# Rounding and subtracting a unit's transposed probabilities in one instruction each

## Chip, cores and metric

The kernel runs on one core of one Trainium2 chip. The metric is the device time of one execution in microseconds; the median of three runs of the kernel before is 1191.67 us (1191.44 to 1194.56).

## What is computed

A decoder of two layers on 512 tokens of width 512 (two sequences of 256). Each step is added to a residual stream `x` after a layer norm: an autocorrelation mix, a quantised cross product with a context, a quantised feed-forward, a grouped-query attention over a gathered key cache, a cross attention over context and latents, and a mixture of eight experts. The change touches the two attentions, which end in

```python
# first: 32 heads, 8 key heads, width 128, 512 cached + 256 new keys
scores = jnp.einsum('bhld,bhtd->bhlt', qh, k_full) / math.sqrt(HD)
attn = jax.nn.softmax(scores, axis=-1)
out = jnp.einsum('bhlt,bhtd->bhld', attn, v_full)
# second: 16 heads, 4 key heads, width 96, 512 context + 256 latent keys
scores = jnp.einsum('bkgqd,bksd->bkgqs', q, k) * scale
attn = jax.nn.softmax(scores.astype(jnp.float32), axis=-1).astype(q.dtype)
out = jnp.einsum('bkgqs,bksd->bkgqd', attn, v)
```

## The kernel before

Every engine (TensorE: PE, ScalarE: ACT, VectorE: DVE, GpSimd: POOL, SyncE: SP) has its own program, written out by hand in the order in which it runs; the engines meet only at semaphores (`s["name"]`), and a wait holds up everything behind it on its engine. Products of full precision are made of three matmuls each (`product`, L1887 to L1889): every operand is split into a rounded part, made by ScalarE as a copy into a rounded type, and a remainder, made by VectorE or GpSimd as a subtraction.

An attention runs over groups, one for each key head: eight groups (0 to 7) in the first attention, four in the second. A group has 16 units: four heads times four tiles of 128 query rows, each against 768 keys. Unit U = 16 g + u goes through the engines like this:

- TensorE, two units ahead: the scores (six matmuls, L1887 to L1889) into one of two pairs of banks.
- VectorE: the row maximum out of PSUM (`row_max`, L1464). ScalarE: the exponential with its row sum (`exps`, L969). VectorE: the reciprocal (`row_sum`, L1469). GpSimd: the product of the two (L673).
- TensorE: the probabilities, 128 x 768, are transposed in six steps of 128 columns (L2018), three into bank 4 and three into bank 5 (`B_PT`).
- ScalarE rounds them into `PTH` (L984); VectorE subtracts the rounded part from PSUM into `PTL` (L1514). Each does this for half a unit, one bank, at a time. The transposes of the next unit overwrite the banks, so each half of them waits for the subtraction of the same half (`pt_out0`, `pt_out1`).
- After the transposes TensorE has other matmuls to do in most units: values times probabilities of a whole head (`head_values`), the next group's queries (`project_q`), the output projection of the group before (`project_out`).

In unit u TensorE's order is: scores of U+2, transposes of U, other matmuls. ScalarE's order is: the roundings of U, a finished head's or query's copy where there is one, the exponential of U+2. VectorE's order is: a low query part (L1479) where one is due, the maximum of U+2, the subtractions of U, the reciprocal of U+2, then rotations of queries (L1445, L1447), a head's remainder (`head_out`, L1485) or the addition of a projected row block (L1491). The tables at the top of the kernel (`Q_UNITS`, `V_UNITS`, `Q_OUT`, `Q_SPLIT`, `V_OUT` and the same with a 2 for the second attention) say in which unit each extra step lies. The first group of an attention has no output projection and no earlier head behind it, and the last one has no queries of a next group.

Of the kernel before, what the change touches and what calls it, by code (L numbers as in the profile page):

```python
# [20 lines left out]
P = 128  # L21
B, S, D = 2, 256, 512
TOK = B * S
RT = TOK // P
# [20 lines left out]
UNITS = GH * RT  # L45
# [27 lines left out]
def decoder_kernel(nc, x, ctx, ctx_t, qscale, wgu, wd, dft, idft, nyq, freqs, wq1, wk1, wv1, wo1,  # L73
                   kcache, vcache, block_idx, wq2, wk2, wv2, wo2, gate_w, expert_w, out):
    es = ExitStack()
    with es:
# [206 lines left out]
        def bank(n):  # L283
            return PS[:, n, :]

        def bankb(n):
# [24 lines left out]
            sc_ready nmax_ready exp_done rsum_ready pn_ready pt_psum pt_out1 pt_out0 ot_psum ot_ev  # L311
# [78 lines left out]
        def fr(ap):  # L390
            return ap.bitcast(FR)
# [11 lines left out]
        def _(sp):  # L403
# [174 lines left out]
            sp.wait_ge(s["pt_psum"], 2 * UNITS * KV1)  # L578
# [133 lines left out]
        def _(act):  # L712
# [229 lines left out]
            def attention(first, groups, rotated, hd, new_values_out, prepare):  # L942
# [29 lines left out]
                def group(g, tail, last):  # L972
                    for u in range(UNITS):
# [8 lines left out]
                        for half in range(2):  # L982
                            act.wait_ge(s["pt_psum"], 2 * U + half + 1)
                            act.activation(fr(PTH[:, (u // 4) % 2, 3 * half:3 * half + 3, u % 4 * P:(u % 4 + 1) * P]),  # L984
                                           bank(B_PT[half])[:, 0:3 * P].rearrange("p (k c) -> p k c", k=3),
                                           ACT.Copy).then_inc(s["pt_hi"], 1)
# [108 lines left out]
        def _(dve):  # L1095
# [362 lines left out]
            def attention(first, groups, rotated, hd, first_rows, last_queries, prepare):  # L1458
# [36 lines left out]
                def group(g, tail, last):  # L1495
                    for u in range(UNITS):
# [14 lines left out]
                        for half in range(2):  # L1511
                            ks = slice(3 * half, 3 * half + 3)
                            dve.wait_ge(s["pt_hi"], 2 * U + half + 1)
                            dve.tensor_tensor(fr(PTL[:, (u // 4) % 2, ks, cols]),  # L1514
                                              bank(B_PT[half])[:, 0:3 * P].rearrange("p (k c) -> p k c", k=3),
                                              PTH[:, (u // 4) % 2, ks, cols], ALU.subtract)\
                               .then_inc(s[f"pt_out{half}"], 1)
# [125 lines left out]
        def _(pe):  # L1643
# [257 lines left out]
            def attention(first, groups, hd, keys, new_values, first_product=None):  # L1901
# [9 lines left out]
                def head_values(g, j, k0=0, k1=KK):  # L1911

                    if k0 == 0:
                        pe.wait_ge(s["pt_out1"], UNITS * g + RT * (j + 1))
                        pe.wait_ge(s["pt_out0"], UNITS * g + RT * (j + 1))
                        pe.wait_ge(s["ot_ev"], GH * g + j)
# [17 lines left out]
                def last_head_values(g, half):  # L1934

                    j = GH - 1
                    if half == 0:
                        pe.wait_ge(s["pt_out1"], UNITS * (g + 1))
                        pe.wait_ge(s["pt_out0"], UNITS * (g + 1))
# [56 lines left out]
                def group(g, tail, last):  # L1996
                    for u in range(UNITS):
# [13 lines left out]
                        pe.wait_ge(s["pn_ready"], U + 1)  # L2011
                        for half in range(2):
                            pe.wait_ge(s[("pt_out0", "pt_out1")[half]], U)
# [6 lines left out]
                            mm.then_inc(s["pt_psum"], 1)  # L2020
# [265 lines left out]
```

## Time and profile before

| | |
|---|---|
| median of the runs | 1191.67 us (1191.44 to 1194.56) |
| the profiled execution | 1190.17 us, its span 1188.3 us |
| PE (matmuls) busy | 1104.0 us, 93% of the span |
| DVE busy | 869.3 us, 73% |
| ACT busy | 607.1 us, 51% |
| POOL busy | 491.7 us, 41% |
| first attention, transposes of units | 262.7 to 785.4 us of the span |
| second attention, transposes of units | 833.4 to 1069.7 us |

The page of a profile adds up what each engine did over the whole span. What an engine waits for, and whether that matters, is read from the views of single stretches: the instructions in order of time with the idle time ahead of each, the chain of waits followed back from the last instruction, and busy time by stretch. Times in those views are counted from the start of the span.

### The profile page before, as it was taken

Reading aid. Unit: us, or ns where it says so; the run is one execution under the profiler, and the core shown is the slowest. Engines: PE = TensorE matmul, PEld = TensorE weight load, DVE = VectorE, ACT = ScalarE, POOL = GpSimd, SP = SyncE. Lnnn points to the kernel's source line nnn. Section 1 sums busy time; section 2 is a strip of 40 time slices with the busy share of each in tenths; the row PEclk is TensorE's granted clock in tenths of the full one; section 3 lists DMA queues with packets and bytes.
Section 4 is the critical chain, followed back from the end, with each engine's and each line's share of the span. In section 5 each row is a group of like instructions: output and inputs, shape, how many; then the busy total and the mean of one; then the engine's idle time right before and its main releaser. Section 6 shows DMA issues by size and latency. Waiting matters only on the chain.

```text
span 1188.3 us, 17689 instructions
## 1 busy us (share of the span) xinstructions
PE 1104.0 (93%) x5871; PEld 882.5 (74%) x5878; DVE 869.3 (73%) x1471; ACT 607.1 (51%) x1236; POOL 491.7 (41%) x360
## 2 busy tenths in 40 slices
PE   3976867899999999999999999999899999999998
PEld 2433333477888888888888888877788989887887
DVE  6999989867867777786868777657676676755434
ACT  2523443436656556565656656553665666553110
POOL 1361000124655645564655545462656565550000
PEclk9798989899999999999999999999999999999999
DMA  9364145220011011101010010142103020111121
GB/s 320 131 200 163 49 129 190 76 85 27 18 50 36 23 53 31 53 18 57 18 57 26 22 35 14 62 106 63 61 18 92 18 60 31 48 36 72 71 106 71
DMA packets 41813, 83.10 MB, mean 70 GB/s; under 512 B 10212, under 2 KB 18917, under 8 KB 38565
## 3 DMA queue, kind: packets, MB, share of 16 engines
q1 hardware_dynamic: 40164, 77.24, 20.1%
q0 software_dynamic: 1600, 5.24, 1.4%
q8 instruction: 28, 0.46, 0.2%
q14 instruction: 21, 0.16, 0.0%
HBM read 71.59 MB, written 10.22 MB: 69 GB/s over the span
## 4 chain that ended last, share of the span: by engine, by line
PE 79%; DVE 12%; issue 4%; ACT 3%; POOL 1%; DMA 1%; SPq 0%; ACTq 0%; DVEq 0%; POOLq 0%
PE PS L1887 21%; PE PS L1889 20%; PE PS L1888 20%; PE PS L2018 9%; PE PS L1704 1%; PE PS L1830 1%; PE PS L1784 1%; ACT arena L969 1%; PE PS L1654 1%; ACT PTH L984 1%; PE PS L1815 1%; PE PS L1673 1%; DVE arena L1238 1%; DVE arena L1115 1%; DVE arena L1126 1%
## 5 line engine op out<-in xcount | busy, mean ns | idle before, releaser
L673 POOL TENSOR_TENSOR arena<-arena,rsum 128x768 f32<-128x768 f32 x192 | 283.1, 1475 | 362.3 <-DVE rsum L1469 362.3
L984 ACT ACTIVATE PTH<-PS 128x384 fp32r<-128x384 f32 x384 | 167.8, 489 | 245.3 <-PE PS L2018 245.0
L1464 DVE TENSOR_REDUCE nmax<-PS 128x1 f32<-128x768 f32 x192 | 182.9, 953 | 116.6 <-PE PS L1889 115.3
L1514 DVE TENSOR_TENSOR PTL<-PS,PTH 128x384 fp32r<-128x384 f32 x384 | 194.3, 547 | 7.8 <-ACT PTH L984 7.2
L969 ACT ACTIVATE arena<-PS,nmax 128x768 f32<-128x768 f32 x192 | 174.3, 908 | 33.5 <-DVE nmax L1464 33.2
L2018 PE MATMUL PS<-identf,arena 128*128 128x128 f32 x1152 | 158.3, 273 | 6.8 <-POOL arena L673 3.4
L2018 PEld LDWEIGHTS PS<-identf,arena 128*128 128x128 f32 x1152 | 130.2, 140 | 10.1 <-POOL arena L673 5.5
L658 POOL TENSOR_TENSOR WQL<-arena,WQH 128x512 fp32r<-128x512 f32 x44 | 59.1, 1345 | 63.9 <-ACT WQH L743 63.9
L1887 PE MATMUL PS<-PTH,VSH 128*128 128x512 f32 (+1 forms) x198 | 81.0, 409 | 2.4 <-DVE OTL L1485 2.0
L1889 PE MATMUL PS<-PTH,VSL 128*128 128x512 f32 (+1 forms) x198 | 76.4, 386 | 0.0
L1887 PE MATMUL PS<-WOH,OTH 128*128 128x512 f32 (+1 forms) x180 | 74.2, 412 | 2.1 <-DVE OTL L1485 2.0
L1888 PE MATMUL PS<-PTL,VSH 128*128 128x512 f32 (+1 forms) x198 | 76.0, 384 | 0.0
L1887 PE MATMUL PS<-HTH,WQH 128*128 128x512 f32 x176 | 73.6, 418 | 1.6 <-issue 1.6
L1469 DVE RECIPROCAL rsum<-psum_exp 128x1 f32<-128x1 f32 x192 | 31.5, 164 | 59.5 <-ACT arena L969 52.3
L1888 PE MATMUL PS<-WOL,OTH 128*128 128x512 f32 (+1 forms) x180 | 71.0, 394 | 0.0
L1889 PE MATMUL PS<-WOH,OTL 128*128 128x512 f32 (+1 forms) x180 | 70.8, 394 | 0.0
L658 POOL TENSOR_TENSOR WOL<-arena,WOH 128x512 fp32r<-128x512 f32 (+1 forms) x48 | 70.0, 1458 | 0.0
L1889 PE MATMUL PS<-HTH,WQL 128*128 128x512 f32 x176 | 69.7, 396 | 0.0
L1888 PE MATMUL PS<-HTL,WQH 128*128 128x512 f32 x176 | 69.5, 395 | 0.0
L1479 DVE TENSOR_TENSOR QTL<-arena,QTH 128x512 fp32r<-128x512 f32 x37 | 62.4, 1686 | 9.6 <-ACT QTH L961 9.6
L1887 PE MATMUL PS<-PTH,VH 128*96 128x256 f32 x192 | 56.3, 293 | 3.5 <-DVE OTL L1485 3.5
L1889 PE MATMUL PS<-PTH,VL 128*96 128x256 f32 x192 | 54.0, 281 | 0.0
(289 smaller groups left out, 2535.1 us busy)
## 6 DMA issues: line engine op xcount, KB each, us to landing
arena<-in_wo SPq DMA_DIRECT2D x12, 1024.0 KB, 4.8
arena<-in_wq SPq DMA_DIRECT2D x44, 256.0 KB, 2.6
arena<-in_expert_w SPq DMA_DIRECT2D x8, 1024.0 KB, 4.8
arena<-in_wgu SPq DMA_DIRECT2D x11, 512.0 KB, 5.3
arena<-v_dram SPq DMA_DIRECT2D x8, 384.0 KB, 3.4
arena<-in_wd SPq DMA_DIRECT2D x4, 704.0 KB, 6.0
arena<-in_ctx SPq DMA_DIRECT2D x4, 512.0 KB, 3.5
arena<-in_ctx_t SPq DMA_DIRECT2D x2, 1024.0 KB, 11.0
```

The costliest lines, as they stand in the source:

```text
L658: pool.tensor_tensor(fr(lo), raw, hi, ALU.subtract).then_inc(s["w_ready"], heads)
L673: pool.tensor_tensor(PR[:, u % 4, :], PR[:, u % 4, :], rsum[:, u % 4:u % 4 + 1].broadcast_to([P, KEYS]), ALU.mult).then_inc(s["pn_ready"], 1)
L969: act.activation(PR[:, slot, :], SC[pair][:, 0:KEYS], ACT.Exp, bias=nmax[:, slot:slot + 1], accum_out=psum_exp[:, slot:slot + 1]).then_inc ...
L984: act.activation(fr(PTH[:, (u // 4) % 2, 3 * half:3 * half + 3, u % 4 * P:(u % 4 + 1) * P]), bank(B_PT[half])[:, 0:3 * P].rearrange("p (k ...
L1464: dve.tensor_reduce(nmax[:, slot:slot + 1], SC[pair][:, 0:KEYS], AX.X, ALU.max, negate=True)\
L1469: dve.reciprocal(rsum[:, slot:slot + 1], psum_exp[:, slot:slot + 1]).then_inc(s["rsum_ready"], 1)
L1479: dve.tensor_tensor(fr(QTL[:, j, :]), QT[:, j, :], QTH[:, j, :], ALU.subtract)\
L1514: dve.tensor_tensor(fr(PTL[:, (u // 4) % 2, ks, cols]), bank(B_PT[half])[:, 0:3 * P].rearrange("p (k c) -> p k c", k=3), PTH[:, (u // 4) % ...
L1887: pe.matmul(out, fr(xh), fr(yh), start=start, stop=False)
L1888: pe.matmul(out, fr(xh), fr(yl), start=False, stop=False)
L1889: return pe.matmul(out, fr(xl), fr(yh), start=False, stop=stop)
L2018: mm = pe.transpose(bank(B_PT[half])[:, k * P:(k + 1) * P], PR[:, u % 4, c * P:(c + 1) * P], identf[:])
```

## The change

The two roundings of a unit become one ScalarE instruction that reads both banks, and the two subtractions one VectorE instruction. The semaphore that tells of finished transposes (`pt_psum`) counts units now and not halves, `pt_hi` likewise, and one of the two signals of the subtraction (`pt_out0`) is gone. The waits that counted halves are rewritten to match, among them one of SP's ahead of the load of a weight of the second attention.

```diff
-            sp.wait_ge(s["pt_psum"], 2 * UNITS * KV1)
+            sp.wait_ge(s["pt_psum"], UNITS * KV1)
...
-                        for half in range(2):
-                            act.wait_ge(s["pt_psum"], 2 * U + half + 1)
-                            act.activation(fr(PTH[:, (u // 4) % 2, 3 * half:3 * half + 3, u % 4 * P:(u % 4 + 1) * P]),
-                                           bank(B_PT[half])[:, 0:3 * P].rearrange("p (k c) -> p k c", k=3),
-                                           ACT.Copy).then_inc(s["pt_hi"], 1)
+                        act.wait_ge(s["pt_psum"], U + 1)
+                        act.activation(fr(PTH[:, (u // 4) % 2, :, u % 4 * P:(u % 4 + 1) * P]
+                                          .rearrange("p (a k) c -> p a k c", a=2)),
+                                       PS[:, B_PT[0]:B_PT[1] + 1, 0:3 * P].rearrange("p a (k c) -> p a k c", k=3),
+                                       ACT.Copy).then_inc(s["pt_hi"], 1)
...
-                        for half in range(2):
-                            ks = slice(3 * half, 3 * half + 3)
-                            dve.wait_ge(s["pt_hi"], 2 * U + half + 1)
-                            dve.tensor_tensor(fr(PTL[:, (u // 4) % 2, ks, cols]),
-                                              bank(B_PT[half])[:, 0:3 * P].rearrange("p (k c) -> p k c", k=3),
-                                              PTH[:, (u // 4) % 2, ks, cols], ALU.subtract)\
-                               .then_inc(s[f"pt_out{half}"], 1)
+                        dve.wait_ge(s["pt_hi"], U + 1)
+                        lo, hi = (t[:, (u // 4) % 2, :, cols].rearrange("p (a k) c -> p a k c", a=2) for t in (PTL, PTH))
+                        dve.tensor_tensor(fr(lo), PS[:, B_PT[0]:B_PT[1] + 1, 0:3 * P]
+                                          .rearrange("p a (k c) -> p a k c", k=3), hi, ALU.subtract)\
+                           .then_inc(s["pt_out1"], 1)
...
                         pe.wait_ge(s["pn_ready"], U + 1)
+                        pe.wait_ge(s["pt_out1"], U)
                         for half in range(2):
-                            pe.wait_ge(s[("pt_out0", "pt_out1")[half]], U)
                             if not tail and u == 0:
                                 pe.wait_ge(s["vn_ev"], v_steps + half + 1)
                             for k in range(3):
                                 c = 3 * half + k
                                 mm = pe.transpose(bank(B_PT[half])[:, k * P:(k + 1) * P],
                                                   PR[:, u % 4, c * P:(c + 1) * P], identf[:])
-                            mm.then_inc(s["pt_psum"], 1)
+                        mm.then_inc(s["pt_psum"], 1)
```

On TensorE, unit 15 of a middle group of the first attention stands like this before (`pn_ready` tells of GpSimd's product; `identf` is the identity that transposes):

```order
L1889 MATMUL PS<-KNH,QTL 128x256
L2018 MATMUL PS<-identf,arena 128x128 [waits pt_out0,pn_ready]
L2018 MATMUL PS<-identf,arena 128x128 x2
L2018 MATMUL PS<-identf,arena 128x128 [waits pt_out1]
L2018 MATMUL PS<-identf,arena 128x128 x2
L1887 MATMUL PS<-HTH,WQH 128x512 [waits w_ready]
```

and like this after:

```order
L1887 MATMUL PS<-KNH,QTL 128x256
L2014 MATMUL PS<-identf,arena 128x128 [waits pt_out1,pn_ready]
L2014 MATMUL PS<-identf,arena 128x128 x5
L1885 MATMUL PS<-HTH,WQH 128x512 [waits w_ready]
L1886 MATMUL PS<-HTL,WQH 128x512
```

The wait of the second three transposes has moved ahead of the first three.

On VectorE, unit 14 of such a group, from the low query part on, before (`pt_hi` tells of the rounding, `sc_ready` of the scores, `exp_done` of the exponential):

```order
L1479 TENSOR_TENSOR QTL<-arena,QTH 128x512 [waits q_hi]
L1463 REGISTER_ALU
L1464 TENSOR_REDUCE nmax<-PS 128x1 [waits sc_ready]
L1513 ISA
L1514 TENSOR_TENSOR PTL<-PS,PTH 128x3x128 [waits pt_hi]
L1513 REGISTER_ALU
L1514 TENSOR_TENSOR PTL<-PS,PTH 128x3x128 [waits pt_hi]
L1469 RECIPROCAL rsum<-psum_exp 128x1 [waits exp_done]
```

and after:

```order
L1479 TENSOR_TENSOR QTL<-arena,QTH 128x512 [waits q_hi]
L1463 REGISTER_ALU
L1464 TENSOR_REDUCE nmax<-PS 128x1 [waits sc_ready]
L1513 TENSOR_TENSOR PTL<-PS,PTH 128x6x128 [waits pt_hi]
L1469 RECIPROCAL rsum<-psum_exp 128x1 [waits exp_done]
```

Two subtractions of three blocks have become one of six, with one wait; what stands around them is in the same order.

## Rows read from the trace of the kernel before

**Rows 1.** Windows: us, then busy us (instructions) per engine, clock, DMA share, GB/s.

```profile
core 0: us, PE busy (x) PEld busy (x) DVE busy (x) ACT busy (x) POOL busy (x), PEclk, DMA share, GB/s
330.00:740.00 410.00, 410.00 (x2223) 350.52 (x2222) 309.19 (x517) 247.10 (x522) 224.24 (x153) 1.00 0.12 36
```

**Rows 2.** Groups by line and shape: busy us, mean ns of one, idle before them.

```profile
L1514 DVE TENSOR_TENSOR PTL<-PS,PTH 128x384 fp32r<-128x384 f32 x384 | 194.3, 547 | 7.8 <-ACT PTH L984 7.2
L1464 DVE TENSOR_REDUCE nmax<-PS 128x1 f32<-128x768 f32 x192 | 182.9, 953 | 116.6 <-PE PS L1889 115.3
L969 ACT ACTIVATE arena<-PS,nmax 128x768 f32<-128x768 f32 x192 | 174.3, 908 | 33.5 <-DVE nmax L1464 33.2
L984 ACT ACTIVATE PTH<-PS 128x384 fp32r<-128x384 f32 x384 | 167.8, 489 | 245.3 <-PE PS L2018 245.0
...
L1005 ACT ACTIVATE VSH<-arena 128x768 fp32r<-128x768 f32 x8 | 6.8, 850 | 0.0
```

**Rows 3.** Instructions in order of time, unit 8 of group 7: start, us, idle before.

```profile
762.45 0.82 PE L2018 MATMUL PS<-identf,arena 128*128 128x128 f32 x6
...
762.97 0.87 ACT L984 ACTIVATE PTH<-PS 128x384 fp32r<-128x384 f32 x2 [2.03 <-PE PS L2018]
...
763.52 1.01 DVE L1514 TENSOR_TENSOR PTL<-PS,PTH 128x384 fp32r<-128x384 f32 x2
...
764.22 0.92 PE L2018 MATMUL PS<-identf,arena 128*128 128x128 f32 x6
766.14 0.47 PE L1887 MATMUL PS<-PTH,VSH 128*128 128x512 f32 x1 [1.01 <-DVE OTL L1485]
```

**Rows 4.** Chain of waits, the same place: start us, us, what.

```profile
758.82 0.66 PE PS L2018 x6
...
762.61 0.34 PE PS L2018 x3
762.97 0.87 ACT PTH L984 x2
...
765.41 0.60 DVE OTL L1485
```

**Rows 5.** Instructions in order of time, units 12 to 15 of group 1.

```profile
382.94 0.88 ACT L984 ACTIVATE PTH<-PS 128x384 fp32r<-128x384 f32 x2 [1.30 <-PE PS L2018]
...
385.31 0.16 DVE L1469 RECIPROCAL rsum<-psum_exp 128x1 f32<-128x1 f32 x1 [0.81 <-ACT arena L969]
...
387.05 0.96 DVE L1464 TENSOR_REDUCE nmax<-PS 128x1 f32<-128x768 f32 x1
...
389.31 1.47 POOL L673 TENSOR_TENSOR arena<-arena,rsum 128x768 f32<-128x768 f32 x1 [1.03 <-DVE rsum L1469]
...
389.59 1.73 DVE L1479 TENSOR_TENSOR QTL<-arena,QTH 128x512 fp32r<-128x512 f32 x1 [0.36 <-ACT QTH L961]
...
390.00 0.82 PE L2018 MATMUL PS<-identf,arena 128*128 128x128 f32 x6
...
392.11 1.00 DVE L1514 TENSOR_TENSOR PTL<-PS,PTH 128x384 fp32r<-128x384 f32 x2
...
393.13 0.82 PE L2018 MATMUL PS<-identf,arena 128*128 128x128 f32 x6
...
396.24 0.81 PE L2018 MATMUL PS<-identf,arena 128*128 128x128 f32 x6
```

**Rows 6.** TensorE in order of time, at its idle stretches in both attentions.

```profile
287.78 0.47 PE L1887 MATMUL PS<-HTH,WQH 128*128 128x512 f32 x1 [1.46 <-issue]
...
784.56 0.92 PE L2018 MATMUL PS<-identf,arena 128*128 128x128 f32 x6 [0.94 <-DVE PTL L1514]
...
840.98 0.82 PE L2018 MATMUL PS<-identf,arena 128*128 128x128 f32 x6
...
854.13 0.88 PE L2018 MATMUL PS<-identf,arena 128*128 128x128 f32 x6 [2.31 <-POOL arena L673]
...
952.38 0.36 PE L1887 MATMUL PS<-PTH,VH 128*96 128x256 f32 x1 [0.49 <-DVE OTL L1485]
...
1071.70 0.47 PE L1887 MATMUL PS<-WOH,OTH 96*128 96x512 f32 x1 [2.00 <-DVE OTL L1485]
```

More of the change, by code:

```diff
@@ L310, in decoder_kernel @@
             ot_half ot_half_hi ot_half_ev q_moved ot_moved q_psum q_cos q_ready vn_psum vn_ev
-            sc_ready nmax_ready exp_done rsum_ready pn_ready pt_psum pt_out1 pt_out0 ot_psum ot_ev
+            sc_ready nmax_ready exp_done rsum_ready pn_ready pt_psum pt_out1 ot_psum ot_ev
             y_psum y_added
@@ L1914, in head_values @@
                         pe.wait_ge(s["pt_out1"], UNITS * g + RT * (j + 1))
-                        pe.wait_ge(s["pt_out0"], UNITS * g + RT * (j + 1))
                         pe.wait_ge(s["ot_ev"], GH * g + j)
@@ L1938, in last_head_values @@
                         pe.wait_ge(s["pt_out1"], UNITS * (g + 1))
-                        pe.wait_ge(s["pt_out0"], UNITS * (g + 1))
                         pe.wait_ge(s["ot_ev"], GH * g + j)
```

## The prediction

> **What bounds the kernel now.** I read first the windows by stage. From 330 to 740 us, the middle of the first attention, TensorE is busy in all 410.00 us, VectorE in 309.19 (75%), ScalarE in 247.10 (60%), and the granted clock is 1.00, the 2.4 GHz level [rows 1]. So there the matmul engine is the bound, time taken off the other two gives nothing back, and the change can only act by making TensorE wait or wait less. It takes no matmul away.
>
> Second, the rows by line and shape, for durations. A rounding of half a unit (ScalarE, L984) takes 0.489 us, a subtraction (VectorE, L1514) 0.547 us, and there are 384 of each [rows 2]. There is no 768-wide row of either. The nearest are the ScalarE copy of 768 columns out of SBUF at 0.850 us, the exponential of 768 columns out of PSUM at 0.908 us, and the VectorE reduction of 768 columns out of PSUM at 0.953 us [rows 2].
>
> Third, the loop that a unit closes, where nothing covers it. In the last group of the first attention unit 8 has no other matmuls than scores: its transposes start at 762.45, the rounding at 762.97, the subtraction at 763.52, the next unit's transposes at 764.22 [rows 3]. That is 0.52 (three transposes and the hand-over) + 0.49 (half 0 rounded) + 0.06 + 0.55 (half 0 subtracted) + 0.15 (hand-over) = 1.77 us, which is 764.22 - 762.45. A unit cannot be followed sooner.
>
> Fourth, the chain of waits, to see where this loop decides. In that group it leaves TensorE after three transposes (762.61, 0.34 us), goes through the two roundings, the exponential and the subtraction of the head's output (L1485) and comes back at 766.14, after 1.01 us of idle [rows 3, 4].
>
> **The change part by part.** The new order is six transposes, then one rounding, then one subtraction, then the next six transposes.
>
> Start. In the chain three transposes take 0.34 us and six 0.66 [rows 4]: the rounding may start 0.33 us later, 0.85 after the transposes instead of 0.52.
>
> Rounding. Removed are two instructions that together last 0.87 us [rows 4]; added is one. I take 0.85 us, the row of the same operation and width. Bounds: 0.91 (the exponential's row), and 0.80, which is the pair's 0.87 less a second start-up of 0.07 (2 x 0.489 - 0.908). So ScalarE ends 0.85 + 0.85 = 1.70 us after the start instead of 0.52 + 0.87 = 1.39: 0.31 us later (0.26 to 0.37). Everything behind it in ScalarE's order (exponential, head output, queries) starts that much later.
>
> Subtraction. The pair lasts 1.01 us [rows 3]. One instruction: 0.95 (the reduction's row); bounds 1.02 (nothing saved) and 0.88 (a start-up of 0.14 saved, 2 x 0.547 - 0.953). It ends at 1.70 + 0.06 + 0.95 = 2.71 instead of 0.52 + 0.49 + 0.06 + 1.02 = 2.09: 0.62 us later (0.50 to 0.75).
>
> Loop. The shortest distance of two units rises from 1.77 to 2.71 + 0.15 = 2.86 us (2.74 to 2.99).
>
> The two waits of the transposes become one ahead of all six. Behind it on TensorE stand the unit's value, query or output products; those wait for nothing else there, so they slip with it. One wait and one signal fewer cost nothing either way: of the six transposes 0.66 us is twice the three's 0.34 within 0.02, so no gap stood between the halves.
>
> Where it reaches TensorE, place by place:
>
> (a) The middle, units 0 to 13 and 15: the next transposes come 3.11 us or more after the last (unit 15: 396.24 - 393.13 [rows 5]), above 2.86. No cost; if the loop grew past 3.1 us these would start to pay.
>
> (b) Unit 14 of groups 0 to 6. A chain runs over three units and no link has room: rounding of unit 12 at 382.94, the exponential behind it, the reciprocal that waited 0.81 us for that exponential, two rotations, the maximum of unit 13 at 387.05 without a wait, its exponential, the rounded queries, the low query part at 389.59 which waited 0.36 us for them, another maximum, the subtraction of unit 14 at 392.11 [rows 5]. It starts 2.11 us after the transposes at 390.00; the next ones come at 393.13, 3.13 later [rows 5]. Today half 0 is free at 2.11 + 0.55 + 0.15 = 2.81, half 1 at 3.26, when the second three want it at 3.46: covered. After: 2.11 + 0.31 + 0.95 + 0.15 = 3.52, so 0.39 us of new wait (0.27 to 0.52). Seven groups: 2.7 us (1.9 to 3.6).
>
> (c) Places where TensorE already waits for what stands behind the rounding on ScalarE: group 0 of the first attention (287.78, 1.46 us idle, the end of a rotation chain that starts with unit 0's rounding) [rows 6], units 5, 8 and 11 of its last group, unit 15 of the first three groups of the second attention (952.38, idle until L1485) [rows 6], units 9 and 12 of its last. These nine pay 0.31 us each: 2.8 us (2.3 to 3.3).
>
> (d) The last unit pair of both attentions, where TensorE waits for a head subtraction queued behind the unit's own (784.56, 0.94 us idle; 1071.70, 2.00 us) [rows 6]: 0.62 each, 1.2 us (1.0 to 1.5).
>
> (e) Units 2 to 6 of the second attention's first group follow each other with scores alone: 854.13 - 840.98 = 13.15 us for five [rows 6]. Five loops of 2.86 are 14.3: 1.15 us (0.55 to 1.8). GpSimd, which ends this stretch today (2.31 us idle before 854.13), gets its reciprocals late by about the same.
>
> Sum: 2.7 + 2.8 + 1.2 + 1.15 = 7.9 us (5.8 to 10.2). The saved 0.02 us of ScalarE and 0.06 of VectorE per unit, 192 times, is 15 us of busy time and lies wholly beside TensorE.
>
> Rows 1 have VectorE at 75% and ScalarE at 60% while TensorE has no idle. The Trainium skill (Perfetto Trace Analysis, Optimizing Scalar/DVE Operations) says that grouping into larger operations helps when the engine is saturated, and that breaking instructions up may finish work sooner when ScalarE or VectorE are not saturated but cause bubbles on other engines. By its second half this change goes the wrong way; the trace agrees as far as neither engine is full. A second page (VectorE: DVE Perf Modes, the TRN2 errata) gives 172 + 768 cycles at 1.2 GHz and 120 + 768 at 0.96 GHz for these two forms, 0.78 and 0.925 us; with those as an estimate the sum would be 6.0 us.
>
> **The rivals.**
>
> The cover holds: the low query part of unit 14 (1.73 us beside a GpSimd multiplication of 1.47 that starts 0.28 us earlier [rows 5]) runs shorter once both move, so (b) vanishes, and GpSimd's order absorbs (e). For it: VectorE is that stretch's tightest engine; against: both start from the same reciprocal and move together. 7.9 - 2.7 - 1.15 = 4.0, at the low ends 3.3 us: 1195.0 to 1195.7.
>
> The wide forms cost what two narrow ones do: 0.98 and 1.09 us, no overlap, for an access that steps over two banks. Rounding 0.44 later, loop 3.13: (b) 4.6, (c) 4.0, (d) 1.8, (e) 2.5, sum 12.9: 1204.6. Against: the exponential reads both banks in one instruction at 0.908.
>
> Faster, the other side: the wait and signal between the halves cost TensorE's sequencer time in every unit that the trace folds into the transposes. It decides from (7.9 + 3.6) / 192 = 0.06 us per unit on; at 0.10 us it gives 19.2 - 7.9 = 11.3 us: 1180.4. Against: the 0.66 and 0.34 above leave 0.02.
>
> **How the numbers follow.** The profiled execution took 1190.17 us, its span 1188.3; the median of the runs is 1191.67, 1.5 more. The forecast is 1198.1 for a profiled execution and 1191.67 + 7.9 = 1199.6 for the median; its own ends are 1197.5 and 1201.9. A measurement of this kernel can tell 0.3%, 3.6 us, from no change.
> Chances: forecast 0.76, cover 0.10, wide forms 0.10, faster 0.04. The range takes in the cover's low end and a third of the wide forms' case: 1194.8 to 1203.0. Faster by over 0.3%: 0.04. Within: half of the cover's case, and 0.05 of the forecast's through scatter of the runs (those of before lie 3.1 us apart), 0.10. Slower: 0.86.
>
> **What would show it.** Right: ScalarE's form at 0.80 to 0.91 us and VectorE's at 0.88 to 1.02, 192 of each; 2.8 to 2.9 us between the two transpose groups of unit 8 in the last group; new idle of about 0.4 us before the transposes of unit 15 seven times, in a stretch that has none now, with the subtraction as what ended it; VectorE some 15 us less busy at the same TensorE work. Wrong: no idle between 330 and 740 us (the cover held), idle also before unit 0 (wide forms), or transposes of a unit that take less than 0.66 us in the chain.

## The result and the profile after

The changed kernel took 1201.32 us, the median of four executions (1197.31 to 1202.04); the kernel before, on the same chip, 1191.74. The ratio is 1.0071, with a 95% interval of 1.0053 to 1.0089: it is slower by 6 to 11 us. A second set of runs, taken with the experiments, gave 1200.39 against 1192.32 us, ratio 1.0065 (1.0050 to 1.0081). The profiled execution took 1197.31 us, its span 1195.5; before they were 1190.17 and 1188.3.

The two instructions came out as they were costed, 192 of each. Groups by line and shape of the changed kernel (count, then busy us, mean ns of one, idle before them), to set beside [rows 2]:

```profile
L1513 DVE TENSOR_TENSOR PTL<-PS,PTH 128x768 fp32r<-128x768 f32 x192 | 183.4, 955 | 72.2 <-ACT PTH L983 71.3
...
L983 ACT ACTIVATE PTH<-PS 128x768 fp32r<-128x768 f32 x192 | 156.0, 813 | 279.4 <-PE PS L2014 279.1
```

The subtraction takes 0.955 us and the rounding 0.813. VectorE is busy 10.9 us less and ScalarE 11.8 us less for these two steps than in [rows 2], and the kernel is slower all the same. Where it became slower stands in the list of what TensorE waited for between 255 and 1190 us (what for, then us in total, how often, the longest). Of the kernel before:

```profile
PE PS L1887 <- DVE OTL L1485: 7.5, 8, 2.0
PE PS L2018 <- POOL arena L673: 3.4, 3, 2.3
PE PS L2018 <- DVE PTL L1514: 3.2, 5, 1.2
```

and of the changed one:

```profile
PE PS L2014 <- DVE PTL L1513: 16.3, 21, 2.0
PE PS L1885 <- DVE OTL L1485: 4.2, 7, 2.6
PE PS L2014 <- POOL arena L673: 1.1, 1, 1.1
```

The transposes (L2014) now wait for the subtraction at 21 places instead of 5. Part of that was there before under other names: the waits for a head's output (OTL) and for GpSimd have shrunk. The three rows add up to 14.1 us before and 21.6 after, 7.5 us more. The other rows of the list shrank from 2.6 to 1.3 us, so the idle time of the whole list rose by 6.2 us. It does not hold the whole cost, as will be seen at unit 15 below.

Unit 8 of group 7 shows the loop, as in [rows 3]; instructions in order of time of the changed kernel (start, us, engine, idle before):

```profile
765.13 0.82 PE L2014 MATMUL PS<-identf,arena 128*128 128x128 f32 x6
...
765.99 0.81 ACT L983 ACTIVATE PTH<-PS 128x768 fp32r<-128x768 f32 x1 [2.09 <-PE PS L2014]
766.69 0.59 ACT L965 ACTIVATE OTH<-PS 128x512 fp32r<-128x512 f32 x1
767.17 0.91 ACT L969 ACTIVATE arena<-PS,nmax 128x768 f32<-128x768 f32 x1
...
766.83 0.96 DVE L1513 TENSOR_TENSOR PTL<-PS,PTH 128x768 fp32r<-128x768 f32 x1 [0.54 <-ACT PTH L983]
768.20 0.16 DVE L1469 RECIPROCAL rsum<-psum_exp 128x1 f32<-128x1 f32 x1 [0.41 <-ACT arena L969]
768.28 0.67 DVE L1485 TENSOR_TENSOR OTL<-PS,OTH 128x512 fp32r<-128x512 f32 x1
...
767.94 0.85 PE L2014 MATMUL PS<-identf,arena 128*128 128x128 f32 x6 [0.93 <-DVE PTL L1513]
769.10 0.47 PE L1885 MATMUL PS<-PTH,VSH 128*128 128x512 f32 x1 [0.31 <-DVE OTL L1485]
```

The rounding starts 0.86 us after the transposes (0.52 before), the subtraction 0.84 after it, and the next unit's transposes start 767.94 - 765.13 = 2.81 us after the last ones, where it was 1.77. TensorE's single wait of 1.01 us for the head's output has become 0.93 for the subtraction and 0.31 for the head's output.

In the middle of the first attention TensorE was never idle before [rows 1]. The same stretch now:

```profile
330.00:740.00 410.00, 408.95 (x2210) 348.55 (x2209) 304.85 (x417) 240.02 (x422) 223.39 (x153) 1.00 0.11 36
```

The 1.05 us that are missing belong to one place in each group, ahead of unit 15's transposes. In group 1, to set beside [rows 5] (VectorE first, then TensorE):

```profile
390.03 1.74 DVE L1479 TENSOR_TENSOR QTL<-arena,QTH 128x512 fp32r<-128x512 f32 x1 [0.35 <-ACT QTH L961]
391.69 0.95 DVE L1464 TENSOR_REDUCE nmax<-PS 128x1 f32<-128x768 f32 x1
392.56 0.94 DVE L1513 TENSOR_TENSOR PTL<-PS,PTH 128x768 fp32r<-128x768 f32 x1
...
390.17 0.82 PE L2014 MATMUL PS<-identf,arena 128*128 128x128 f32 x6
...
393.06 0.29 PE L1886 MATMUL PS<-KNL,QTH 128*128 x1
393.19 0.28 PE L1887 MATMUL PS<-KNH,QTL 128*128 x1
393.65 0.84 PE L2014 MATMUL PS<-identf,arena 128*128 128x128 f32 x6 [0.18 <-DVE PTL L1513]
```

The idle column says 0.18 us, yet the distance of the two transposes is 393.65 - 390.17 = 3.48 us and was 3.13: 0.35 more. The row of 393.19 is why: its 0.28 us is the time from its start to its modelled end, while back-to-back matmuls of this form start every 0.12 to 0.13 us (393.06 to 393.19). Idle is counted from that end, so some 0.17 us of each such wait is not in the idle column. In this kernel waits are better sized from distances between starts, and so are the sums in the next section.

### The profile page after: what moved, and what is told of

The parts are those of the page before. It is cut to its first block, busy times and chain, and to the rows that moved or that the text cites. A ratio compares the mean times of both kernels' runs of the same rounds, so it can differ in the third digit from the quotient of the medians.

```text
span 1195.5 us, 16802 instructions
## 1 busy us (share of the span) xinstructions
PE 1105.4 (92%) x5878; PEld 883.3 (74%) x5878; DVE 859.7 (72%) x1279; ACT 594.8 (50%) x1044; POOL 491.8 (41%) x360
## 4 chain that ended last, share of the span: by engine, by line
PE 74%; DVE 15%; issue 5%; ACT 5%; POOL 1%; DMA 1%; ACTq 0%; DVEq 0%; SPq 0%; POOLq 0%
PE PS L1885 19%; PE PS L1887 19%; PE PS L1886 19%; PE PS L2014 9%; ACT arena L969 2%; DVE nmax L1464 1%; PE PS L1702 1%; PE PS L1828 1%; PE PS L1782 1%; DVE PTL L1513 1%; ACT PTH L983 1%; PE PS L1652 1%; DVE arena L1445 1%; DVE arena L1447 1%; PE PS L1671 1%
## 5 line engine op out<-in xcount | busy, mean ns | idle before, releaser
L983 ACT ACTIVATE PTH<-PS 128x768 fp32r<-128x768 f32 x192 | 156.0, 813 | 279.4 <-PE PS L2014 279.1
L1513 DVE TENSOR_TENSOR PTL<-PS,PTH 128x768 fp32r<-128x768 f32 x192 | 183.4, 955 | 72.2 <-ACT PTH L983 71.3
L2014 PE MATMUL PS<-identf,arena 128*128 128x128 f32 x1152 | 157.7, 273 | 17.5 <-DVE PTL L1513 16.3
L2014 PEld LDWEIGHTS PS<-identf,arena 128*128 128x128 f32 x1152 | 129.9, 140 | 21.8 <-issue 20.4
```

The source lines that it names most:

```text
L983: act.activation(fr(PTH[:, (u // 4) % 2, :, u % 4 * P:(u % 4 + 1) * P] .rearrange("p (a k) c -> p a k c", a=2)), PS[:, B_PT[0]:B_PT[1] + 1 ...
L1513: dve.tensor_tensor(fr(lo), PS[:, B_PT[0]:B_PT[1] + 1, 0:3 * P] .rearrange("p a (k c) -> p a k c", k=3), hi, ALU.subtract)\
L2014: mm = pe.transpose(bank(B_PT[half])[:, k * P:(k + 1) * P], PR[:, u % 4, c * P:(c + 1) * P], identf[:])
```

## Where the 7 us are

The transposes of every unit have a start time in both traces, so the difference between the kernels can be followed from unit to unit. From the first transposes of the first attention to the first output product after the last unit (262.74 to 1071.70 us before, 261.09 to 1078.82 after) the changed kernel needs 8.77 us more. Of that 1.3 us are seven matmuls of group 0 that ran at TensorE's lower clock level; 7.4 us are waits:

| place | forecast, us | measured, us |
|---|---|---|
| (b) unit 14 and 15, groups 0 to 6 | 2.7 | 2.5 |
| (c) nine places behind ScalarE's order | 2.8 | 2.3 |
| (d) the last unit pair of both attentions | 1.2 | 1.4 |
| (e) units 2 to 6 of the second attention's first group | 1.15 | 1.26 |
| (a) everything else | 0 | 0.0 |
| sum | 7.9 | 7.4 |

The second profile of the changed kernel gives the same numbers within 0.05 us at each place (group 0 and its clock apart). The waits of (d) and (e) in the first one:

```profile
786.07 0.85 PE L2014 MATMUL PS<-identf,arena 128*128 128x128 f32 x6
788.90 0.85 PE L2014 MATMUL PS<-identf,arena 128*128 128x128 f32 x6 [1.98 <-DVE PTL L1513]
789.50 0.47 PE L1885 MATMUL PS<-WOH,OTH 128*128 128x512 f32 x1
...
859.33 0.88 PE L2014 MATMUL PS<-identf,arena 128*128 128x128 f32 x6 [1.12 <-POOL arena L673]
...
1078.82 0.47 PE L1885 MATMUL PS<-WOH,OTH 96*128 96x512 f32 x1 [2.58 <-DVE OTL L1485]
```

They answer to 784.56, 854.13 and 1071.70 in [rows 6], with 0.94, 2.31 and 2.00 us. At (e) the wait for GpSimd became shorter since four waits of 0.93 to 1.01 us for the subtraction now stand ahead of it; the stretch as a whole went from 13.15 to 14.41 us.

At (d) in the first attention the row of 784.56, which the prediction names, is a wait for the unit's own subtraction. The head's subtraction behind it releases the first output product, which stands in these rows of the kernel before:

```profile
782.80 0.82 PE L2018 MATMUL PS<-identf,arena 128*128 128x128 f32 x6
...
785.62 0.47 PE L1887 MATMUL PS<-WOH,OTH 128*128 128x512 f32 x1
```

From the transposes of unit 14 to that product it was 2.82 us (782.80 to 785.62) and is 3.43 (786.07 to 789.50). At the end of the second attention it went from 2.81 us, between the last transposes and 1071.70, to 3.43. So each of the two places pays 0.61 us for the head's subtraction; the rest of the 1.4 us lies close around the first place.

## Experiments: which part of the change costs

Three kernels each contain one part of the change. The first rounds both banks in one instruction and keeps the two subtractions with their two signals.

```diff
-for half in range(2):
-    act.wait_ge(s["pt_psum"], 2 * U + half + 1)
...
+act.wait_ge(s["pt_psum"], U + 1)
...
+               PS[:, B_PT[0]:B_PT[1] + 1, 0:3 * P].rearrange("p a (k c) -> p a k c", k=3),
+               ACT.Copy).then_inc(s["pt_hi"], 1)
...
-    dve.wait_ge(s["pt_hi"], 2 * U + half + 1)
+    dve.wait_ge(s["pt_hi"], U + 1)
```

> Undoes half of the change: one rounding over both banks behind six transposes, but two subtractions of half a unit each, and TensorE waits for each half apart. Theory (what counts is when ScalarE's rounding and VectorE's last subtraction end, place by place): against the kernel before, the rounding ends 0.27 us later and both subtractions 0.62 us later, half 0 is free 0.31 us earlier than in the changed kernel, so the loop is 0.85 + 0.81 + 0.04 + 0.55 + 0.15 = 2.40 us. Unit 14: half 0 free 3.08 us after its transposes, covered by 3.13; half 1 at 3.54 where it is wanted at 3.46, about 0.08 us in each of seven groups, 0.5 us. Nine places behind ScalarE's order 0.27 each, 2.4 us. Last unit pairs 0.62 each, 1.2 us. Second attention's first group: five loops of 2.40 fit into 13.15, 0 to 0.3 us. Sum about 4.3 us, ratio 1.0036. Rival one (the single subtraction with its single wait is the whole cost): within 1 us of before. Rival two (waiting with the rounding for six transposes is the whole cost): 7 us or more, as the changed kernel.

Measured: 1198.03 against 1192.32 us, ratio 1.0052 (1.0037 to 1.0066). The forecast of 4.3 us (1.0036) lies just below the interval. From the first transposes to the first output product after the last unit the profile has 5.3 us more, so neither rival (1 us; 7 us or more) fits. The loop measured 2.41 us (764.32 to 766.73) where 2.40 was expected:

```profile
764.32 0.82 PE L2018 MATMUL PS<-identf,arena 128*128 128x128 f32 x6
766.73 0.92 PE L2018 MATMUL PS<-identf,arena 128*128 128x128 f32 x6 [0.53 <-DVE PTL L1514]
```

By place it paid 0.3 us at (b), 1.6 in group 7, 0.7 at (e), where 0 to 0.3 was expected, and 2.5 in the rest of the second attention, 0.56 of it at a place where the trace names a DMA (below). Without that it is 4.7 us.

The second part alone: two roundings, one subtraction over both banks behind them, one wait of TensorE.

```diff
-for half in range(2):
-    dve.wait_ge(s["pt_hi"], 2 * U + half + 1)
...
+dve.wait_ge(s["pt_hi"], 2 * U + 2)
...
+dve.tensor_tensor(fr(lo), PS[:, B_PT[0]:B_PT[1] + 1, 0:3 * P]
+                  .rearrange("p a (k c) -> p a k c", k=3), hi, ALU.subtract)\
+   .then_inc(s["pt_out1"], 1)
...
+pe.wait_ge(s["pt_out1"], U)
 for half in range(2):
-    pe.wait_ge(s[("pt_out0", "pt_out1")[half]], U)
```

> The other half alone: two roundings of half a unit each, as before, one subtraction over both banks behind the second, one wait of TensorE ahead of six transposes. Theory: ScalarE's order is not moved, so the nine places behind it pay nothing. The subtraction starts at 1.40 + 0.05 and ends at 2.40 us after the transposes (2.09 before, 2.66 in the changed kernel); loop 2.55 us. Unit 14: 2.11 + 0.95 + 0.15 = 3.21 against 3.13, 0.08 us in each of seven groups, 0.5 us. Last unit pairs 0.31 each, 0.6 us. Five loops of 2.55 fit into 13.15. Sum about 1.1 us, ratio 1.0009. Rival one (the subtraction is the whole cost): 7 us or more. Rival two: nothing at all, within 0.5 us of before.

Measured: 1194.46 us, ratio 1.0016 (1.0008 to 1.0025), 1 to 3 us. The waits are 2.35 us: 0.6 at (b), 0.5 in group 7, 0.5 at (e), 0.8 in the rest, 0.5 of that again at the DMA's place. Without it 1.8 us, where 1.1 was expected; the 0.5 at (e) is most of what was missing. The loop measured 2.54 us, expected 2.55.

The third changes no instruction of ScalarE or VectorE; TensorE only waits for both halves ahead of all six transposes.

```diff
+pe.wait_ge(s["pt_out0"], U)
+pe.wait_ge(s["pt_out1"], U)
 for half in range(2):
-    pe.wait_ge(s[("pt_out0", "pt_out1")[half]], U)
```

> The kernel before with one edit: TensorE waits for both subtracted halves ahead of all six transposes; roundings and subtractions stay as halves. Theory: loop 2.09 + 0.15 = 2.24 us instead of 1.77, with ScalarE's and VectorE's ends unmoved by themselves. Unit 14: 2.11 + 1.01 + 0.15 = 3.27 against 3.13, 0.14 us in each of seven groups, 1.0 us; where TensorE then waits behind ScalarE's order the later transposes push the rounding behind them, at most 0.14 us at each of nine places, since half 1 waits there already; the rest fits. Sum 1.0 to 2.0 us, ratio 1.0008 to 1.0017. Rival (losing the overlap of the halves' transposes is the main cost): 5 us or more, ratio over 1.004.

Measured: 1193.48 us, ratio 1.0016 (1.0005 to 1.0026). The loop is 2.23 us, expected 2.24. The profile has 2.8 us more than before between the same two points, of which some 1.5 us lie in group 0 with a stretch at the lower clock level; the waits are about 1.3 us, 1.0 of them at unit 14 and 15 of groups 0 to 6, as expected. The rival (5 us or more) fell.

So the loop followed the ends of the instructions in every variant: 1.77, 2.23, 2.41, 2.54 and 2.81 us for the kernel before, the wait alone, the rounding alone, the subtraction alone and the whole change. The larger part of the cost comes with the rounding that waits for six transposes, 4.7 us against 1.8 for the single subtraction. About half of it, 2.3 us, lies at the nine places behind ScalarE's order, where the single subtraction alone pays nothing: ScalarE's following work moves with the rounding.

At one place of the second attention a DMA may add something to the comparison. In the profile of the subtraction alone:

```profile
905.56 0.50 PE L1885 MATMUL PS<-WOH,OTH 128*128 128x512 f32 x1 [0.25 <-DMA OTL<-OTL]
```

Three profiles have this row (both parts of the change alone and a later variant), with 0.47 to 0.56 us more between the transposes around it than before. In four other variants the same distance is 0.15 to 0.24 us longer without such a row, and in the remaining profiles, those of the two kernels compared among them, it is unchanged. What causes it stays open.

## Experiments: why the runs of one kernel differ by 4 us

The timed runs of the changed kernel lay 4 us above its profiled one. It was run again unaltered.

> The changed kernel unaltered, for a second profile: its timed runs were 4 us above its profiled one (1201.3 against 1197.3). Theory one (the granted clock falls to its lower level at some of the enlarged waits, not at the same ones in every execution): ratio 1.006 to 1.008, and the profile shows stretches at granted clock 0.50 behind waits, between 260 us and the end, that differ from those of the first profile (286 to 289 us), each some 1 to 2 us long in lost time. Theory two (the waits themselves are longer in those runs): the places before the transposes of units 14, 5, 8 and 11 of the last group would be longer than in the first profile, by some 0.1 us each in all 30 or so places. Theory three (the part before the first attention, up to 260 us, differs): the first transposes of the attention start later than 262.7 us.

Measured: 1200.39 us, ratio 1.0065 (1.0050 to 1.0081); the span of the second profile is 1200.2 us, 4.7 more than the first. The waits are the same (theory two fell). Three places make the difference: 1.5 us before 262 us (what theory three is about), 0.2 in group 0, 3.0 behind the last wait of the second attention (theory one). Windows of the first profile (the number behind the engines is the granted clock):

```profile
core 0: us, PE busy (x) PEld busy (x) DVE busy (x) ACT busy (x) POOL busy (x), PEclk, DMA share, GB/s
284.00:286.00 2.00, 0.85 (x6) 0.64 (x6) 1.70 (x4) 0.44 (x2) 1.28 (x1) 0.96 0.00 0
286.00:288.00 2.00, 1.71 (x4) 1.46 (x5) 1.30 (x3) 1.78 (x3) 0.53 (x2) 0.50 0.00 0
```

and of the second, with the first output products in order of time:

```profile
1080.00:1085.00 5.00, 4.51 (x11) 3.58 (x12) 1.02 (x2) 1.91 (x1) 0.00 (x0) 0.53 0.80 334
...
1080.49 0.76 PE L1885 MATMUL PS<-WOH,OTH 96*128 96x512 f32 x1 [2.58 <-DVE OTL L1485]
```

Behind a wait of 2.58 us TensorE came back at granted clock 0.50, the 1.2 GHz level, and its matmul of 0.47 us took 0.76. The first profile has the same wait of 2.58 us and no lower clock behind it (its 1078.82 row above has 0.47). In the part before 262 us the first profile has granted clock 1.00 from 215 to 230 us, the second and the kernel before 0.89 there; those are the 1.5 us.

The kernel before was run again for a second profile too.

> The kernel before unaltered, for a second profile. Theory (the spread of its runs, 1189.6 to 1195.0 us, is the granted clock at its lower level behind waits, at other places in each execution): the span exceeds the lowest by the time lost in stretches at granted clock 0.50, each behind a wait of 0.9 us or more (284 to 288, 784.6, 854.1, 1071.7 us) or in the part before 260 us; the transposes come at the same distances as in the first profile elsewhere. Rival (the waits themselves vary): the distances between transposes differ from the first profile at several places without a change of clock.

Measured: 1193.14 us, span 1191.3, that is 3.0 more than in its first profile, and again the distances of the transposes agree except behind two waits:

```profile
855.00:860.00 5.00, 5.00 (x30) 4.82 (x29) 1.54 (x4) 1.40 (x5) 3.11 (x3) 0.66 0.00 0
1075.00:1080.00 5.00, 5.00 (x24) 4.14 (x23) 2.29 (x1) 1.91 (x1) 0.00 (x0) 0.79 0.43 175
```

The clock fell behind the waits of 2.31 and 2.00 us and cost 1.5 and 1.6 us. So the two profiles of each kernel differ by the clock, and a wait costs its length plus, in some executions, this. That the other timed runs scatter for the same reason is likely but not shown: of those only the mean granted clock of the whole execution is on record, and it does not follow their times (for the kernel before 0.979 at 1189.61 us and 0.980 at 1193.26).

## Experiments: are the places what they were said to be

Three edits are each aimed at the cause of one group of places. In the first, head 2's low query part is taken in unit 1 of the next group instead of unit 14, so that in unit 14 VectorE has no work ahead of the maximum.

```diff
-Q_SPLIT = {8: 0, 11: 1, 14: 2}
+Q_SPLIT = {8: 0, 11: 1}
...
+if tail and not first and u == 1:
+    queries_lo(g, 2)
```

> The changed kernel with one VectorE instruction moved: the low part of head 2's queries (first attention) is taken in unit 1 of the next group instead of unit 14. Theory (the new wait ahead of unit 15's transposes comes from VectorE's order in unit 14, where that low part stands ahead of the maximum and the subtraction): the subtraction of unit 14 starts about 1.70 us after its transposes, as in other units, instead of 2.37, and is done at 2.66; loop 2.86 is below 3.13, the wait of 0.33 us in each of seven groups is gone, 2.3 us less than the changed kernel (about 1198.1 against 1200.4; ratio to before about 1.0045). The first attention's middle then has no TensorE idle. Rival (the wait comes from the wide forms' loop in itself, or from GpSimd): the places stay, ratio 1.0065.

Measured: 1198.07 against 1190.94 us, ratio 1.0048 (1.0033 to 1.0063). The window 330 to 740 us has no idle again, and the transposes of all units of groups 1 to 6 come at the same distances as before the change, within 0.02 us. Units 14 and 15 of group 1 have their transposes at 391.49 and 394.62, 3.13 us apart as before:

```profile
330.00:740.00 410.00, 410.00 (x2220) 350.81 (x2219) 300.41 (x420) 240.33 (x424) 221.35 (x153) 1.00 0.11 36
...
391.69 0.96 DVE L1464 TENSOR_REDUCE nmax<-PS 128x1 f32<-128x768 f32 x1 [0.69 <-PE PS L1889]
393.19 0.96 DVE L1515 TENSOR_TENSOR PTL<-PS,PTH 128x768 fp32r<-128x768 f32 x1 [0.54 <-ACT PTH L983]
...
391.49 0.82 PE L2016 MATMUL PS<-identf,arena 128*128 128x128 f32 x6
394.62 0.82 PE L2016 MATMUL PS<-identf,arena 128*128 128x128 f32 x6
```

VectorE now waits 0.54 us for the rounding in unit 14, and the subtraction starts 1.70 us after the transposes at 391.49, as in other units. So term (b) was VectorE's order.

The second edit moves a head's subtraction ahead of the reciprocal that waits for the exponential; it was made on both kernels.

```diff
+if u in v_out:
+    head_out(g, v_out[u])
 if scored:
     row_sum(U + 2, (u + 2) % 4)
...
-if u in v_out:
-    head_out(g, v_out[u])
```

> The same move on the kernel before. Theory: there VectorE idles up to 0.7 us between the unit's subtraction (ended 2.08 us after the transposes) and the reciprocal, so the head's output is subtracted that much earlier; TensorE's idle of 0.99 to 1.01 us at four places in the last groups falls by about 0.75 each, the 0.45 to 0.58 us at the end of three groups of the second attention by about 0.3 each: 3.9 us less than before, ratio 0.9967. Rival (the reciprocal, later by 0.6 us, makes GpSimd late, and TensorE waits for the normalised probabilities instead): no gain, ratio 0.999 to 1.001.

Measured: 1188.09 us, ratio 0.997 (0.9958 to 0.9981). On the kernel before it takes away TensorE's waits for the head's output at all seven places, 4.7 us by the distances of the transposes (0.84 to 0.88 at the four long ones, 0.39 to 0.45 at the three short ones). In the place of [rows 3]:

```profile
764.05 0.68 DVE L1485 TENSOR_TENSOR OTL<-PS,OTH 128x512 fp32r<-128x512 f32 x1
764.85 0.16 DVE L1469 RECIPROCAL rsum<-psum_exp 128x1 f32<-128x1 f32 x1
...
763.82 0.92 PE L2018 MATMUL PS<-identf,arena 128*128 128x128 f32 x6
764.88 0.47 PE L1887 MATMUL PS<-PTH,VSH 128*128 128x512 f32 x1
```

The value product starts 1.06 us after the transposes, where it was 1.92. On the changed kernel:

> The changed kernel with the subtraction of a head's output moved ahead of the reciprocal that waits for the exponential, on VectorE. Theory (in the changed kernel VectorE's subtraction of the unit ends at 2.66 us, after ScalarE's exponential at 1.70 + 0.90, so the reciprocal waits for nothing any more): the head's output comes only about 0.1 us earlier, at seven places, at most 0.7 us less than the changed kernel, ratio to before 1.006 to 1.0065. Rival (TensorE's waits there are still set by the exponential): 0.3 us or more each, 2 us or more in all, ratio below 1.005.

Measured: 1196.83 us, ratio 1.0041 (1.0025 to 1.0057), and by the distances 3.3 us less waiting, 0.38 to 0.54 at each of the seven places. My expectation of 0.7 us fell and its rival stood. I had left out ScalarE's copy of the head's output: in the rows of unit 8 above it lies between rounding and exponential (766.69, 0.59 us), so the exponential ends at 768.08 and the reciprocal of 768.20 waited 0.41 us for it.

The third edit puts the first half of the last head's value products ahead of the output products that wait for head 2; its wait for the subtractions counts up to unit 13 now, which is all that it reads.

```diff
-LAST_OT = (B_OT, 3)
+LAST_OT = (3, B_OT)
...
+last_head_values(g, 0)
 for r in range(2):
     project_out(g, r, LAST_BANKS[r], range(GH - 1), last=True)
-last_head_values(g, 0)
```

> The changed kernel with the value products of the first half of the last head moved ahead of the output products that wait for head 2, into bank 3 (the second half takes the bank of the head outputs), in both attentions. They need units 12 and 13 only, so they fill TensorE's last wait in the second attention (2.58 us in both profiles of the changed kernel) with 18 products of 0.12 us. Theory one (waiting, and the lower clock level that follows that wait): idle there falls to about 0.4 us, 2.1 us less; no stretch at granted clock 0.50 behind it, which cost 3.1 us in the second profile of the changed kernel and nothing in the first; 3 to 4 us less on the median of the runs, ratio to before 1.003 to 1.004. Theory two (the clock falls there whatever TensorE does): only the 2.1 us, and a stretch at 0.50 in the profile at 1075 to 1090 us. Theory three (the filler moves the wait to the next products): no gain, ratio 1.0065.

Measured: 1196.70 us, ratio 1.0044 (1.0030 to 1.0057). The wait fell from 2.58 to 0.46 us, and the clock behind it is 1.00:

```profile
1080.01 0.47 PE L1885 MATMUL PS<-WOH,OTH 96*128 96x512 f32 x1 [0.46 <-DVE OTL L1485]
...
1080.00:1085.00 5.00, 5.00 (x22) 4.09 (x23) 1.43 (x1) 2.18 (x2) 0.00 (x0) 1.00 0.69 285
```

That is the expected 2.1 us for certain; the 2.5 us between this ratio and the 1.0065 of the changed kernel has an uncertainty of about 2 us, and doesn't tell whether the clock added to it. Nor does the one profile exclude theory two: the first profile of the changed kernel had no lower clock there either.

Last, the edits together. On the kernel before, the two that help it:

> The kernel before with both moves that helped: the head output's subtraction ahead of the reciprocal, and the first half of the last head's value products ahead of the output products that wait for head 2. Theory (they act at different places, so they add up): the move on VectorE measured 4.7 us by its seven places; the filler takes about 1.9 us of the last wait of 2.00 us. Together 6 to 6.6 us less than before, ratio 0.9945 to 0.995; no stretch at granted clock 0.50 behind the last wait of the second attention. Rival (the filler was worth its 2 us only because the changed kernel's gap was longer and the clock fell there): ratio 0.9965 to 0.9975, as the move on VectorE alone.

Measured: 1185.15 against 1191.09 us, ratio 0.995 (0.9936 to 0.9964): 6 us faster than the kernel before, the fastest of all. The two moves add up: its profile has 4.7 us less at the seven places and 1.5 us less behind the last unit. On the changed kernel, all three:

> The changed kernel with the three moves: head 2's low query part in unit 1 of the next group, the head output's subtraction ahead of the reciprocal, and the filler ahead of the last output products. Theory (the wide forms cost only where TensorE waits, place by place, and the places add up): against before 7.4 us of waits, less 2.4, 3.4 and 2.1: within 1 us of before apart from the clock, ratio 0.999 to 1.001; and 6 us slower than the kernel before with two of these moves. Rival (the moves overlap: one wait gone shows the next, as the 0.93 us ahead of the transposes in the last groups): ratio 1.002 to 1.003.

Measured: 1190.69 us, ratio 0.9989 (0.9977 to 1.0001). With three covers put back the wide forms are level with the kernel before, as the sum of the places said, and 5.5 us behind the same kernel with narrow forms and two of the moves. Its largest row of TensorE's waits is the loop of 2.81 us itself; below it stands the same row of the kernel with narrow forms and two of the moves:

```profile
PE PS L2017 <- DVE PTL L1515: 15.1, 14, 2.0
PE PS L2019 <- DVE PTL L1514: 3.2, 5, 1.1
```

The difference of the rows is more than the 5.5 us, since other waits shrink where this one grows (those for GpSimd from 3.6 to 1.1 us).

## Why the prediction was right, step by step

**The bound.** Right: 22.7 us less work on VectorE and ScalarE bought nothing. Nowhere in the profile of the changed kernel does TensorE gain by it: where two transposes came 0.4 us or more closer together, those just ahead of them had come apart by as much or more.

**Rounding and subtraction.** 0.81 us for a forecast of 0.85 (0.80 to 0.91), 0.955 for 0.95. The nearest rows, ScalarE's copy and VectorE's reduction of the same width, priced them within 0.04 us. The 15 us that I expected VectorE to be less busy are, by my own figures, the sum of both engines (0.06 and 0.02 us in 192 units make 11.5 and 3.8); the subtractions lost 10.9 us and the roundings 11.8. The Trainium skill (Perfetto Trace Analysis, Optimizing Scalar/DVE Operations) says that breaking instructions up may finish work sooner when these engines are not full but cause bubbles on others; the trace agrees: the narrow forms cost 22.7 us more busy time in all and yet close the loop in 1.77 us instead of 2.81.

**The loop.** 2.81 us for 2.86, the 0.05 being the shorter rounding.

**(a)** Right: the middle units keep their distances, units 0 to 13 within 0.02 us.

**(b)** Right in place and mechanism (the edit that moved the low query part removed it), 2.5 us for 2.7. What I said would show it, idle of about 0.4 us, was wrong as a reading: the idle column shows 0.16 to 0.19, and the distance of the starts 0.32 to 0.35.

**(c)** Mis-sized: 2.3 us for 2.8. Each place paid 0.24 to 0.28 us, since the rounding ends 0.27 us later and not 0.31; group 0 paid about 0.2, the rest being absorbed within the group.

**(d)** 1.4 us for 1.2, inside its bounds; the head's subtraction behind the unit's own cost 0.61 us at each of the two places, for 0.62. The row of 784.56 that I gave for the first of them shows another wait, as said above.

**(e)** 1.26 us for 1.15, right in place and size, but not by the sum that I made. Five loops do not set this stretch: with the rounding alone five of 2.41 us and with the subtraction alone five of 2.54 fit into its 13.15 us, and yet it paid 0.72 and 0.46. GpSimd sets it. In each kernel one of its products waits there for the reciprocal; here in the kernel before, the rounding alone, the subtraction alone and the changed kernel:

```profile
845.61 1.47 POOL L673 TENSOR_TENSOR arena<-arena,rsum 128x768 f32<-128x768 f32 x1 [0.61 <-DVE rsum L1469]
...
849.42 1.47 POOL L673 TENSOR_TENSOR arena<-arena,rsum 128x768 f32<-128x768 f32 x1 [1.04 <-DVE rsum L1469]
...
846.96 1.47 POOL L673 TENSOR_TENSOR arena<-arena,rsum 128x768 f32<-128x768 f32 x1 [1.10 <-DVE rsum L1469]
...
850.58 1.47 POOL L673 TENSOR_TENSOR arena<-arena,rsum 128x768 f32<-128x768 f32 x1 [1.36 <-DVE rsum L1469]
```

From there GpSimd works for 8.5 us without a pause (8.75 in the changed kernel, with one more wait of 0.21) until its last product releases the transposes that end the stretch, at 854.13 before and 859.33 after. Counted from the first transposes of the stretch, the product above starts 4.63, 5.38, 5.12 and 5.66 us later. The clause that GpSimd gets its reciprocals late by about the same was what held; that five loops gave nearly the same number is luck.

**The sum.** 7.4 us of waits for 7.9. The profiled execution was forecast at 1198.1 us and took 1197.31. That it came so near is luck in part: it gained 1.65 us before 262 us and lost 1.3 in group 0 through the clock, which the prediction didn't have. The median was forecast at 1199.6 us and came out at 1201.32. The medians of the two sets differ by 9.6 and 8.1 us, the ratios (1.0071 and 1.0065 on 1192) say 8.5 and 7.7; whether the longer waits also bring the lower clock more often, for about 1 us, is within the intervals and stays open.

**The rivals.** The cover did not hold: (b) was paid, with the low query part as long as before (1.74 us for 1.73), and GpSimd's order did not absorb (e). The wide forms cost less than two narrow ones (0.81 against 0.87, 0.955 against 1.01 to 1.02); and the removed wait gave nothing that can be seen, since the distances of units 0 to 13 in the middle are unchanged to 0.02 us.

## What to carry to other kernels

One wide instruction in place of two narrow ones saves part of a start-up, here 0.06 us of each pair, but it starts when its last input is there and frees its buffers when all of it is done; where the buffer is single and another engine waits to refill it, add up the new loop from the ends of the instructions and compare it with the shortest distance at which that engine comes back. Then go through the places where the waiting engine stands behind the longer instruction in another engine's order, since these pay even when the loop itself fits. And look there for work that stands in the wrong order: here one subtraction moved ahead of a reciprocal and one block of matmuls moved into a wait were worth 6 us, against the 7.4 us of waits that the change brought.

## What was not expected of the hardware

TensorE's clock after a wait is not the same in every execution. In thirteen profiles of eleven kernels the granted clock fell to 0.50 behind the two waits of group 0 near 284 to 288 us in eight, behind a last wait of 2.0 to 2.6 us in the second attention in five of ten, behind GpSimd's 2.3 us near 852 us in three of four, and behind the 1.98 us at the end of the first attention in two of six; each time it cost 1.3 to 3.0 us. Where the filler had cut the last wait to 0.46 us or moved it (three profiles) it did not fall there; beside five of ten that is too few to call the filler the reason. The same wait in another execution of the same kernel left the clock at 1.00.

Idle time of TensorE in these views is counted from a modelled end of the last matmul, and left out some 0.17 us of each wait ahead of unit 15.
